# Cross attention 3 in units of a head pair and half of the queries; in cross attention 0 VectorE adds the last second-half exponentials

## The reference

```python
q = split_heads(Q @ Wq.T + bq)          # 1024 queries, 16 heads of 8
k = split_heads(K @ Wk.T + bk)          # 6404 keys
v = split_heads(V @ Wv.T + bv)
scores = einsum('bhqd,bhkd->bhqk', q, k) / sqrt(8)
scores = where(mask == 0, -1e9, scores)
attn = softmax(scores, axis=-1)
ctx = einsum('bhqk,bhkd->bhqd', attn, v)
return ctx @ Wo.T + bo                   # added to x
```

## Time and profile before

| | us |
|---|---|
| median of 3 runs | 5889.34 |
| lowest and highest | 5887.56, 5891.16 |
| the profiled execution, its time | 5890.79 |
| the profiled execution, its span | 5889.0 |
| PE busy | 5275.3 |
| VectorE (DVE) busy | 2752.2 |
| ScalarE (ACT) busy | 3176.3 |
| GpSimd (POOL) busy | 2217.9 |

### The profile page before, as it was taken

How to read it: one execution, slowest core, us unless ns; L and a number is a source line. 1 busy time by engine, 2 the same in 40 slices (tenths; PEclk the granted TensorE clock), 3 DMA queues, 4 the chain that set the end, 5 groups by cost and what they waited for, 6 DMA issues and landing times. The chain is left out here.

```text
span 5889.0 us, 69174 instructions
## 1 busy us (share of the span) xinstructions
PE 5275.3 (90%) x27886; PEld 1716.5 (29%) x27886; DVE 2752.2 (47%) x3206; ACT 3176.3 (54%) x3203; POOL 2217.9 (38%) x1113
## 2 busy tenths in 40 slices
PE   6869999999999999988989689999886788888889
PEld 2213333333333333333244311111342111111123
DVE  6664455454545453014541410000246999988723
ACT  3355545555555555521022389999224677777861
POOL 1108898989898899924634000000000000000000
PEclk7859999999999999999999799999896799999999
DMA  1000000000000000000000120000203000000010
GB/s 50 15 0 1 1 1 1 1 1 1 1 1 1 1 1 1 1 20 22 2 0 4 39 96 10 20 11 2 77 27 118 18 11 11 11 11 11 7 45 31
DMA packets 64432, 100.75 MB, mean 17 GB/s; under 512 B 9846, under 2 KB 49880, under 8 KB 62000
## 3 DMA queue, kind: packets, MB, share of 16 engines
q1 hardware_dynamic: 63906, 95.50, 4.8%
q10 hardware_dynamic: 206, 0.83, 0.0%
HBM read 70.85 MB, written 25.31 MB: 16 GB/s over the span
## 5 line engine op out<-in xcount | busy, mean ns | idle before, releaser
L2434 ACT ACTIVATE Pr<-ps,key_bias 128x1024 f32<-128x1024 f32 x816 | 892.8, 1114 | 1015.4 <-PE ps L2326 1013.4
L2522 DVE TENSOR_REDUCE red<-ps 128x2 f32<-128x1024 f32 (+1 forms) x767 | 907.6, 1185 | 959.8 <-PE ps L2311 954.5
L2580 POOL TENSOR_TENSOR Ps<-Ps,Pr 128x1024 f32<-128x1024 f32 x400 | 946.0, 2365 | 215.9 <-ACT Pr L2434 215.9
L2589 POOL TENSOR_TENSOR Ps<-Ps,Pr 128x1024 f32<-128x1024 f32 x400 | 947.7, 2369 | 0.0
L3207 DVE TENSOR_REDUCE red<-ps 128x1 f32<-128x512 f32 (+3 forms) x1024 | 877.4, 907 | 95.7 <-PE ps L3080 76.0
L3163 ACT ACTIVATE Pr<-ps 128x1024 f32<-128x1024 f32 x816 | 786.2, 1021 | 228.2 <-PE ps L3090 227.3
L2324 PE MATMUL ps<-Q,Kr 64*128 64x512 f32 x3264 | 841.9, 594 | 0.5 <-DVE red L2522 0.2
L2343 PE MATMUL ps<-Pr,Vc 128*64 128x512 f32 x3264 | 790.0, 605 | 0.0
L3337 ACT ACTIVATE Pr<-ps 128x2048 f32<-128x2048 f32 x467 | 726.5, 2029 | 3.4 <-PE ps L3300 3.3
L3080 PE MATMUL ps<-Kp,Q 52*128 52x512 bf16 (+1 forms) x1664 | 442.6, 412 | 170.6 <-DVE red L3207 124.9
L3103 PE MATMUL ps<-Pr,V 128*9 128x512 f32 x3264 | 436.1, 606 | 0.0
(11 more groups left out here) (578 smaller groups left out, 5219.0 us busy)
## 6 DMA issues: line engine op xcount, KB each, us to landing
L_dram_K<-parts SPq DMA_DIRECT2D x26, 384.0 KB, 3.2
Kp<-L_dram_K SPq DMA_DIRECT2D x14, 624.0 KB
L_dram_K<-parts SPq DMA_DIRECT2D x26, 256.0 KB, 2.9
wB<-L_ffn_shares SPq DMA_DIRECT2D x1, 6144.0 KB
w<-L_ffn_experts_w_dram SPq DMA_DIRECT2D x24, 256.0 KB
Kp<-L_dram_K SPq DMA_DIRECT2D x14, 416.0 KB
wB<-L_ffn_shares SPq DMA_DIRECT2D x1, 3584.0 KB, 12.7
ctx<-ctx_dram SPq DMA_DIRECT2D x13, 256.0 KB, 7.5
```

The source lines that it names most:

```text
L2434: nc.scalar.activation(Pr[:, t % 4, half].rearrange("p a n -> p (a n)"), ps[:, 2 * half:2 * half + 2, :].rearrange("p a n -> p (a n)"), AC ...
L2522: nc.vector.tensor_reduce(red[:, g // C % 2, q, :, g % C], ps[:, maxima_bank(g, s, steps, q):maxima_bank(g, s, steps, q) + 2, 0:ctx.keys_i ...
L2580: nc.gpsimd.tensor_tensor(into, into, src, ALU.add).then_inc(*summed0.up())
L2589: nc.gpsimd.tensor_tensor(into, into, src, ALU.add).then_inc(*summed1.up())
```

## The change

In cross attention 0 VectorE takes the second-half adds of the last 8 key tiles, `t` = 400 to 407.

```diff
+    late = KT * P - 8
...
@@ -2520,6 +2522,11 @@
                     if g >= 2 * C and g % C == 0 and q == 0:
                         nc.vector.wait_ge(*rows_step.at(3 * (g // C) - 4))
                     nc.vector.tensor_reduce(red[:, g // C % 2, q, :, g % C], ps[:, maxima_bank(g, s, steps, q):maxima_bank(g, s, steps, q) + 2, 0:ctx.keys_in(g % C)], AX, ALU.max).then_inc(*reduced.up())
+                t = KT * (j // C) + TPC * (j % C) + s
+                if j < N and t >= late:
+                    nc.vector.wait_ge(*exp_done.at(2 * t + 2))
+                    nc.vector.wait_ge(*summed1.at(t))
+                    nc.vector.tensor_tensor(Ps1[:, j // C % 2], Ps1[:, j // C % 2], Pr[:, t % 4, 1], ALU.add).then_inc(*summed1.up())
...
@@ -2579,8 +2586,11 @@
                         nc.gpsimd.wait_ge(*summed0.at(t))
                         nc.gpsimd.tensor_tensor(into, into, src, ALU.add).then_inc(*summed0.up())
                     into, src = Ps1[:, j // C % 2], Pr[:, t % 4, 1]
-                    nc.gpsimd.wait_ge(*exp_done.at(2 * t + 2))
-                    if t % KT == 0:
+                    if t < late:
+                        nc.gpsimd.wait_ge(*exp_done.at(2 * t + 2))
+                    if t >= late:
+                        pass
+                    elif t % KT == 0:
                         if t >= 2 * KT:
                             nc.gpsimd.wait_ge(*sums_mm.at(j // C - 1))
                         nc.gpsimd.tensor_copy(into, src).then_inc(*summed1.up())
...
-        self.O = dram("O", (self.H, self.dv, S), F32)
+        self.O = dram("O", (self.H, 2, self.dv, S) if softmax else (self.H, self.dv, S), F32)
...
-        self.per_fetch, self.per_query, self.early_chunks = (6, 4, 3) if softmax else (2, 2, 3)
+        self.per_fetch, self.per_query, self.early_chunks = (6, 4, 5) if softmax else (2, 2, 3)
```

```diff
-    P, C, KT = 8, ctx.chunks, ctx.tiles
-    N, LAG = P * C, C + 1
+    W, C, KT = 16, ctx.chunks, ctx.tiles
+    N, LAG, DT = W * C, C + 1, (KT + 1) // 2
...
-    red, neg, shift = k.tile(stack, "red", [128, 2, 16, C]), k.tile(stack, "neg", [128, 8, 2]), k.tile(stack, "shift", [128, 16])
-    by_act = (1, 2, 4, 5, 6, 7)
+    red, neg, shift = k.tile(stack, "red", [128, 2, 8, C]), k.tile(stack, "neg", [128, 4, 2]), k.tile(stack, "shift", [128, 8])
+    by_act = (1, 2, 3)
...
-    out = SmallOutput(k, A, X, Oc, stack)
+    out = SoftmaxOutput(k, A, X, Oc, stack)
...
     def turns():
         for g in range(N + LAG + 1):
-            j = g - LAG
-            yield g, j, (ctx.tiles_in(j % C) if 0 <= j < N else TPC)
+            yield g, g - LAG
+    def key_tiles(t):
+        return range(2 * (t % DT), min(KT, 2 * (t % DT) + 2))
...
     def units(i):
         if i < LAG:
-            return [(2 * q, 2, (4, 0, 2)[(8 * i + q) % 3]) for q in range(8)]
-        sizes = (2, 1, 2, 1, 2, 1, 2, 1, 2, 1, 1) if (i - LAG) % 2 == 0 else (1, 2, 1, 2, 1, 2, 1, 2, 1, 2, 1)
-        return [(sum(sizes[:u]), n, 4 if (u + i - LAG) % 2 == 0 else 7) for u, n in enumerate(sizes)]
+            return [(2 * q, 2, (4, 0, 2)[(4 * i + q) % 3]) for q in range(4)]
+        sizes = (1, 2, 1, 2, 1, 1)
+        return [(sum(sizes[:u]), n, (7, 4)[u % 2]) for u, n in enumerate(sizes)]
...
+        fetch(1)
+        fetch(2)
+        for w in range(W - 2):
+            nc.sync.wait_ge(*out_copied.at(w + 1))
+            for x in range(2):
+                for a in range(2):
+                    at = 32 * (2 * x + a)
+                    nc.sync.dma_start(A.O[2 * (w // 2) + a, x, :, HALVES[w % 2]], Oc[at:at + 9, w % 2, :]).then_inc(*out_stored[w % 2].dma())
+            if w % 2:
+                p = w // 2
+                if p + 3 < W // 2:
+                    fetch(p + 3)
+                for stored in out_stored:
+                    nc.sync.wait_ge(*stored.dmas(4 * (p + 1)))
+                out.sp_load(p)
...
+        def scores(t, x):
+            w = t // DT
+            p, kt = w // 2, 2 * (t % DT) + x
+            if kt == 0:
+                nc.tensor.wait_ge(*rows_set.at(2 * w + 2))
+            take_banks(2 * x, exp_done.at(exp_number(t, x)))
             for a in range(2):
-                mm = nc.tensor.matmul(ps[:, 2 * half + a, :], lhsT=Kp[head(a), p % 3, kt * 128:(kt + 1) * 128], rhs=Q[head(a), p, HALVES[half]], start=True, stop=True)
+                mm = nc.tensor.matmul(ps[:, 2 * x + a, :], lhsT=Kp[head(a), p % 3, kt * 128:(kt + 1) * 128], rhs=Q[head(a), p, HALVES[w % 2]], start=True, stop=True)
             mm.then_inc(*scored.up())
...
+            w = t // DT
+            if t % DT == 0:
+                if w:
+                    nc.tensor.wait_ge(*out_copied.at(w))
                 nc.tensor.matmul(ps[:, 6, :], lhsT=zero_row[:, 0:128], rhs=zero_row[:], start=True, stop=True, skip_group_check=True)
-            for half in range(2):
-                nc.tensor.wait_ge(*exp_done.at(2 * t + half + 1))
+            for x, kt in enumerate(key_tiles(t)):
+                nc.tensor.wait_ge(*exp_done.at(exp_number(t, x)))
                 for a in range(2):
-                    at = 32 * (2 * half + a)
-                    mm = nc.tensor.matmul(ps[at:at + 9, 6, :], lhsT=A.V[:, kt, 2 * p + a, :], rhs=Pr[:, t % 4, half, a, :], start=False, stop=True, skip_group_check=True)
+                    at = 32 * (2 * x + a)
+                    mm = nc.tensor.matmul(ps[at:at + 9, 6, :], lhsT=A.V[:, kt, 2 * (w // 2) + a, :], rhs=Pr[:, t % 4, x, a, :], start=False, stop=True, skip_group_check=True)
             mm.then_inc(*weighed.up())
...
-        def rows(p):
-            nc.tensor.wait_ge(*rows_step.at(3 * p + 3))
-            take_banks(4, rows_set.at(2 * p + 2))
-            for q in range(8):
+        def rows(w):
+            nc.tensor.wait_ge(*rows_step.at(3 * w + 3))
+            take_banks(4, rows_set.at(2 * w + 2))
+            for q in range(4):
                 for a in range(2):
-                    mm = nc.tensor.matmul(ps[64 * a + 32:64 * a + 34, 4 + q // 4, (q % 4) * 128:(q % 4 + 1) * 128], lhsT=mz[:, q, a, :], rhs=k.consts.ident16[:], start=True, stop=True)
+                    mm = nc.tensor.matmul(ps[64 * a + 32:64 * a + 34, 4, q * 128:(q + 1) * 128], lhsT=mz[:, q, a, :], rhs=k.consts.ident16[:], start=True, stop=True)
...
+        for g, j in turns():
+            for s in range(2):
+                t, items = 2 * C * (j // C) + 2 * (j % C) + s, maxima_at(g, s)
+                there = len(key_tiles(t)) if 0 <= j < N else 0
                 for u in items[:1]:
                     maxima(g, u)
-                if 0 <= j < N:
-                    scores(j, s, 0)
+                if there:
+                    scores(t, 0)
                 for u in items[1:2]:
                     maxima(g, u)
-                if 0 <= j < N:
-                    scores(j, s, 1)
+                if there > 1:
+                    scores(t, 1)
                 for u in items[2:]:
                     maxima(g, u)
                 if g == N + 1 and s == 0:
                     nc.tensor.wait_ge(*taken[7])
                     out.pe_bias()
+                if g == N + 3 and s == 0:
+                    out.pe_sums(0, out_copied.at(W - 1))
                 if j == N - 1 and s == 0:
                     nc.tensor.wait_ge(*taken[4])
-                    out.pe_pairs(4)
-                if j >= 0 and 0 < t <= KT * P and (j < N or s == 0):
+                    out.pe_pairs()
+                    out.pe_last(0)
+                if j >= 0 and 0 < t <= DT * W and (j < N or s == 0):
                     products(t - 1)
                 if s == 1 and g % C == 0 and 0 < g <= N:
                     rows(g // C - 1)
-        out.pe_last(4, out_copied.at(P))
+        out.pe_sums(1, out_copied.at(W))
+        out.pe_last(1)
```

The output part, in the new class `SoftmaxOutput`:

```diff
+        for half, sl in enumerate(HALVES):
+            v.wait_ge(*self.sums_mm.at(half + 1))
+            v.reciprocal(self.inverse[:], ps[:, 7, :]).then_inc(*self.scaled.up())
+            v.wait_ge(*self.scaled.at(4 * half + 2))
+            v.tensor_tensor(self.Oc[:, half, :], self.Oc[:, half, :], self.inverse[:], ALU.mult).then_inc(*self.scaled.up())
+            if half == 0:
+                v.wait_ge(*self.scaled.at(1))
+                v.wait_ge(*self.over_in.dmas(1))
+                for s in HALVES:
+                    v.tensor_tensor(self.U[0:n, 0, s], self.U[0:n, 0, s], self.over[0:n, s], ALU.mult).then_inc(*self.scaled.up())
             v.wait_ge(*self.out_mm.at(half + 1))
-            if self.A.softmax:
-                v.scalar_tensor_tensor(X[:, sl], self.k.ps[:, bank + half, :], self.bias[:, 0:1], X[:, sl], ALU.add, ALU.add).then_inc(*self.x_added.up())
-            else:
-                v.tensor_tensor(X[:, sl], X[:, sl], self.k.ps[:, bank + half, :], ALU.add).then_inc(*self.x_added.up())
+            v.scalar_tensor_tensor(X[:, sl], ps[:, 4 + half, :], self.bias[:, 0:1], X[:, sl], ALU.add, ALU.add).then_inc(*self.x_added.up())
...
+    def pe_sums(self, half, copied):
+        t = self.k.nc.tensor
```

(49 more changed lines are left out.)

227 lines of the change are left out of this document (104 added, 123 removed).

## The result

The changed kernel takes **5930.44 us** (median of 4 runs, 5925.06 to 5935.94), the kernel before 5890.25 beside it (5887.56 to 5893.73): ratio **1.0068**, 95% interval 1.0055 to 1.0081. It is 40 us slower, where 5907 (17.6 slower) had been forecast. The profiled execution spans 5933.3 us, 44.3 more than the 5889.0 of before.

What follows compares the result with a forecast made beforehand. The kernel is a chain of twelve layers, so a stage's time is the kernel's. -46.0 + 120.7 - 49.3 - 9.2 = +16.2 us gave 5905.5; with small left-out terms 5907 us, range 5889 to 5932.

Steps and rivals of the forecast that it cites:

- start: Cross attention 3's opening with maxima alone: each engine's work halves, 92.0 becomes 46.0 us, so -46.0.
- middle: Cross attention 3 between first and last row computations: 15 spans of 71.2 us, 1068.0 against 947.3, so +120.7.
- tail: Cross attention 3's end with exponentials alone: 51 instead of 102 exponentials follow the last rows; together -49.3 us.
- cross attention 0: End of that stage: VectorE takes the last 8 second-half adds, so PE's sums start earlier and run shorter; -9.2 us.
- full turn: In the middle: six VectorE reductions in 4.89 us and a gap of 0.58, 5.47 us start to start.
- Rival C: In the middle's turns: the gap does not come, a turn is 4.89 us, kernel faster at 5803; chance 0.07.
- Short turn: In each middle span: two PE steps, 4.0 us, plus 0.55 us for row reductions and subtraction.
- calm handover: Between spans, from rows to scores: VectorE idles 1.63 us, 1.05 of it new, without a clock loss.
- Rival B: The clock falls at each handover, price 1 to 2 us, 15 times: 5922 to 5937 us; chance 0.17.
- forecast case: Case A for the whole kernel: gap at every turn, calm handovers, 5895 to 5918 us; chance 0.56.
- Rival D: Handover and short turn are cheaper by 1.2 us, 15 times: 5889 us, no change; chance 0.17.
- Rival E: In the middle PE falls to the low clock for good: about 6390 us; chance 0.03.

Runs made afterwards that it cites:

- experiment 3: The kernel before with only the cross attention 0 change (VectorE takes the last eight second-half adds): 5879.80 us, ratio 0.9983.
- experiment 1: The changed kernel with a turn's units in the order 1, 2, 1, 1, 1, 2 items instead of 1, 2, 1, 2, 1, 1: 5822.77 us.
- experiment 2: The changed kernel with a turn's units in the order 1, 1, 1, 2, 1, 2, the three singles in mid-turn: 5914.65 us, one run.
- experiment 11: The changed kernel with each products matmul taking only the first 256 of 512 columns of the exponentials: 5860.29 us.
- experiment 4: The changed kernel with four unread filler matmuls on PE before the scores that wait for the copied rows, at each handover: 5912.30 us, ratio 1.0037.
- experiment 6: The changed kernel, own turn order, with the rows moved ahead of the products and into bank 5 at the 16 handovers: 5898.04 us, ratio 1.0014.
- experiment 7: The kernel before with eight unread filler matmuls behind the rows at each of its 8 handovers: 5875.69 us, ratio 0.9977.
- experiment 5: The changed kernel with turn order 1, 2, 1, 1, 1, 2 and, at handovers, rows ahead of the products in bank 5: 5805.95 us, ratio 0.9855.
- experiment 12: The changed kernel with one more ScalarE copy of 1024 columns ahead of the copies into the queries at each handover: 5958.34 us.

## Why the prediction was right or wrong

| term | forecast | measured | how |
|---|---|---|---|
| start | -46.0 | -45.2 | 92.0; 4517.9 to 4564.7 |
| middle | +120.7 | +149.4 | 947.3; 4564.7 to 5661.4 |
| tail | -49.3 | -48.9 | last row reduction to the next layer's first matmul: 5568.3 to 5685.4; 5661.4 to 5729.6 |
| cross attention 0 | -9.2 | -9.5 | from the last exponentials, as in experiment 3 |
| sum | +16.2 | +45.8 | spans: +44.3, the other stages being 1.5 shorter |

**The full turn was right.** 5.47 had been read from the earlier trace rows, 5.48 it is. Experiments 1, 2 and 11 show that its reason was right too: the gap goes with the order of the sizes around the products, moves with it, and shrinks with the products' length. Rival C had the right lever but not the right kernel: of its 104 us (180 gaps of 0.58) experiment 1 collects 92.

**Short turn and calm handover were right within 0.25.** 4.0, 0.55 and 1.05 were forecast, 5.6 together. 71.45 less 12 times 5.48 is 5.7. The split was less exact than the sum: VectorE's two gaps are 0.89 and 0.88, where 0.08 and 1.55 had been put.

**The step that failed** is the one that took the handovers as calm. Rival B, "the clock falls at each handover", had a chance of 0.17, and its mechanism is the one that came: the clock falls at about half of the handovers and costs 3.5 us in most of these. B's price, 1 to 2 us at every handover, fits the total (25.0 in 15 spans is 1.7 each) though not the way it is spread, which is luck. The argument against B was that PE's idle piece shrinks from 2.13 to about 1.2. It shrank further, to 0.96, and still did not suffice. The argument looked at the length of one pause; another of 0.90 stands 2.0 us ahead of it. With the 0.96 filled or gone and the 0.90 left (experiments 4 and 6) no handover loses the clock. Experiment 4 gives 5912.3, 23.5 us above the 5888.8 of before beside it, inside the forecast case's 5895 to 5918. Of the 28.7 us by which the middle exceeds its forecast, 25.0 are these losses (the first span included) and 3.75 the 0.25 in 15 spans.

**The range held by B.** The measured 5930.4 lies within 5889 to 5932 only because the range took in most of rival B; the forecast case alone ended at 5918, and two of the four executions (5935.07 and 5935.94) lie above the range.

**The baseline hid the price.** The middle of the kernel before was taken as it is, 947.3. It held about 13 us of such losses (experiment 7: 934.2 from first to last row reduction). They were in the number, but not seen as 1.5 to 2.9 for each handover; read so, B would have had a higher chance.

**Cross attention 0** came 0.3 better. The Trainium skill, "SBUF — State Buffer", section "Who interferes with whom", states that a VectorE instruction with two SBUF inputs contends with a GpSimd instruction that reads SBUF. This trace agrees: VectorE's last add takes 2.42 instead of 1.22, and 1.09 of it lie behind the end of GpSimd's (2532.32). The -8.4 that the prediction worked out by that rule were too low a gain all the same: it let VectorE wait for a whole add of 2.42, and GpSimd's last add had begun 1.03 ahead of VectorE's, so that only 1.33 of it were left.

**Rivals D and E** did not come. Over the middle the clock stays at 0.96. Of the 1.2 less at each handover that D wanted, experiments 5 and 6 reach 0.9 (70.5 instead of 71.45), but by moving the rows.

**What stays open** is what decides which handover loses the clock at a wait of 0.96. In the changed kernel neighbouring handovers with the same rows differ, and the two other orders of units lose the clock seldom at the same wait (one and three of 14). The length of one pause doesn't decide it: 0.90 without the 0.96 costs nothing in experiment 6, and in experiment 11 the clock falls behind a pause of 0.53 where PE has less to do in every turn. Nor does their sum alone: experiment 2 has pauses of 0.90, 0.45 and 0.96 within 5 us at its handovers and loses the clock at one of 14. Whether it is the amount of work between the pauses or their place in time, no run here separates. The Trainium skill, "TensorE: Matmul & The Clock Gate", Part 1, lets the clock follow how busy PE has been; experiments 4, 11 and 12 agree in direction, and no run here shows more than that.
